# Four building steps' keys compared in one 16-bit operation, and GpSimd's waits moved onto semaphore increments

## The reference, cut to what matters

```python
agg = jax.ops.segment_sum(h[src], dst, num_segments=n)            # convolution
msgs = transformed[etypes, src]                                    # recurrent cell, 4 edge types
a = jax.ops.segment_sum(msgs, dst, num_segments=num_nodes)
# the message network, per edge, both directions:
edge_in_f = jnp.concatenate([node_states[from_idx], node_states[to_idx], edge_features], axis=-1)
msgs_f = _mlp2(edge_in_f, W1_f, b1_f, W2_f, b2_f)
agg = agg + jax.ops.segment_sum(msgs_r, from_idx, num_segments=n_nodes)
```

## Time and profile before

| | us |
|---|---|
| median of 3 runs | 14334.22 (14333.57 to 14341.42) |
| the profiled execution | 14337.0 |
| its span, first to last instruction | 14335.3 |
| busy: PE, DVE, POOL, ACT | 11014.9, 6087.1, 4602.6, 3500.8 |
| building, first step's product to the last | 334.8 to 3152.2 |
| message stage, GpSimd's first gather to its last scatter | 4649.6 to 10099 |

### The profile page before, as it was taken

How to read it: one execution, slowest core, us unless ns; L and a number is a source line. 1 busy time by engine, 2 the same in 40 slices (tenths; PEclk the granted TensorE clock), 3 DMA queues, 4 the chain that set the end, 5 groups by cost and what they waited for, 6 DMA issues and landing times.

```text
span 14335.3 us, 276563 instructions
## 1 busy us (share of the span) xinstructions
PE 11014.9 (77%) x60459; PEld 6477.5 (45%) x60460; DVE 6087.1 (42%) x28514; ACT 3500.8 (24%) x9549; POOL 4602.6 (32%) x4343
## 2 busy tenths in 40 slices
PE   2666666659997777676776767677789999999999
PEld 2333333333333555555555555555644444444443
DVE  6999999875653333333333333333210000000000
ACT  0545455543330222222222222222100000000000
POOL 2000000000000788888888888888100000000000
PEclk8667766769998899999999999999599999999999
DMA  2333333342216233333333333333589899899898
GB/s 92 116 112 116 112 116 112 112 127 85 98 72 266 37 41 42 41 42 41 41 41 41 41 41 41 41 41 41 44 314 342 327 344 341 329 342 344 328 340 301
DMA packets 1120446, 2096.56 MB, mean 146 GB/s; under 512 B 372941, under 2 KB 982880, under 8 KB 1012496
## 3 DMA queue, kind: packets, MB, share of 16 engines
q1 hardware_dynamic: 823736, 1913.57, 37.9%
q0 software_dynamic: 295904, 174.34, 11.5%
HBM read 1630.27 MB, written 457.23 MB: 146 GB/s over the span
## 4 chain that ended last, share of the span: by engine, by line
PE 50%; issue 21%; POOL 15%; DVE 9%; DMA 1%; DVEq 1%; SPq 1%; ACT 1%; POOLq 0%; ACTq 0%; another core or an unknown queue 0%
PE ps L1484 16%; POOL G L493 8%; PE ps L1489 8%; PE ps L1132 7%; POOL reverse L816 6%; PE ps L1187 4%; DVE hots L1810 2%; DVE hots L1812 2%; PE ps L1178 2%; DVE hots L1811 2%; PE ps L1426 1%; PE ps L1336 1%; PE ps L1287 1%; POOL scatter_hold L815 1%; DMA reverse<-SD,sidx 1%
## 5 line engine op out<-in xcount | busy, mean ns | idle before, releaser
L816 POOL DMA_INDIRECT reverse<-SD,sidx x1660 | 2653.9, 1599 | 389.7 <-issue 378.4
L1132 PE MATMUL ps<-hots 128*128 128x392 f16 x4859 | 1711.4, 441 | 1108.5 <-DVE hots L1812 567.7
L1484 PE MATMUL ps<-chunk,feat 128*128 128x512 f16 (+1 forms) x10192 | 2278.9, 375 | 14.4 <-DVE feat L2161 13.4
L493 POOL DMA_INDIRECT G<-h_table,idx x1660 | 1654.4, 997 | 493.2 <-issue 490.4
L2015 DVE TENSOR_TENSOR acc<-acc,ps 128x132 f32 x1660 | 484.6, 292 | 3094.3 <-PE ps L1350 3014.0
L846 ACT ACTIVATE stagebuf<-ps 128x392 f32 x3248 | 1439.5, 508 | 1414.2 <-PE ps L1135 1347.4
L1347 PE MATMUL ps<-MS,OH 128*128 128x128 f32 x3320 | 781.3, 319 | 1256.2 <-issue 910.9
L1484 PEld LDWEIGHTS ps<-chunk,feat 128*128 128x128 bf16 x10192 | 942.9, 98 | 1342.7 <-issue 349.5
L2121 DVE SCALAR_TENSOR_TENSOR gate_t<-ps,early,gate_rz 64x512 f32<-64x512 f32 (+1 forms) x52 | 37.1, 713 | 3228.1 <-ACT gate_rz L992 3228.1
L1812 DVE TENSOR_SCALAR hots<-count_hi,key_hi 128x294 f16<-128x294 f16 x4859 | 1401.3, 288 | 0.0
L923 ACT ACTIVATE SD<-ps 128x129 f32<-128x129 f32 x1660 | 463.2, 279 | 3803.2 <-DMA reverse<-SD,sidx 3792.6
(11 more groups left out here) (418 smaller groups left out, 15179.4 us busy)
## 6 DMA issues: line engine op xcount, KB each, us to landing
chunk<-adj SPq DMA_DIRECT2D x720, 1792.0 KB, 9.0
adj<-stagebuf SPq DMA_DIRECT2D x406, 784.0 KB, 5.6
chunkA<-adj SPq DMA_DIRECT2D x48, 1792.0 KB, 6.7
chunk<-adj SPq DMA_DIRECT2D x60, 1232.0 KB, 6.9
G<-in_edge SPq DMA_DIRECT2D x1660, 32.0 KB
G<-h_table,idx POOLq DMA_INDIRECT x1660
reverse<-SD,sidx POOLq DMA_INDIRECT x1660
reverse<-acc SPq DMA_DIRECT2D x4, 3225.0 KB, 20.0
```

Source lines behind the costliest of these rows:

```text
L493: nc.gpsimd.indirect_dma_start(G[:, j, 0:width], None, table, bass.IndirectOffsetOnAxis(idx[:, j:j + 1], 0))\
L816: nc.gpsimd.indirect_dma_start(reverse[j % R], bass.IndirectOffsetOnAxis(sidx[:, j:j + 1], 0), SD[:, j % R, :], None, compute_op=ALU.add). ...
L1132: nc.tensor.matmul(ps[:, bass.ds(held["banks"][j % STEPW] >> 12, 2 * COMBS)], hots[:, j % BRING, 0:P], hots[:, j % BRING, P:P + 2 * COMBS] ...
L1484: nc.tensor.matmul(bank[k % 2][:, 0:cols], feat[0][:, hi, 0:2, :].rearrange("p a d -> p (a d)"), columns(chunk4, i % DRING, m, cols), star ...
```

## The change

VectorE handles four steps at once. The ring holds four groups of four steps, with the four steps as the innermost dimension: the element for column c of step s lies at place 4c + s. Keys and counts are 16-bit floats; the counts are repeated four times in SBUF. Three `tensor_tensor` comparisons a group, of 512, 392 and 1176 elements, take the place of twelve `tensor_scalar`; the second operand is four keys, read again for each column. TensorE reads stationary and moving columns with a step of four elements (8 bytes). The key without its type is made in 16 bits. `hot_made` counts groups. On GpSimd both dummy operations become a semaphore increment, without a wait for their own predecessor; the other waits stay.

```diff
+HG = 4
+HGROUPS = -(-BSTEPS // HG)
+HRING = BRING // HG
...
-        key_u = early[:, 0:BPAD]
+        key_u = early[:, 0:BPAD // 2].bitcast(F16)
...
-        key_lo = here("key_lo", [P, BPAD])
-        key_hi = here("key_hi", [P, BPAD])
+        key_lo = here("key_lo", [P, BPAD], F16)
+        key_hi = here("key_hi", [P, BPAD], F16)
...
-        count_lo = here("count_lo", [P, P], F16)
-        count_hi = here("count_hi", [P, 2 * COMBS], F16)
+        count_lo = here("count_lo", [P, P, HG], F16)
+        count_hi = here("count_hi", [P, 2 * COMBS, HG], F16)
...
-        hots = here("hots", [P, BRING, P + 2 * COMBS], F16)
+        hots = here("hots", [P, HRING, P + 2 * COMBS, HG], F16)
...
-        hots_f = stagebuf[:, 0:2 * BPAD].bitcast(F32)
+        hots_f = stagebuf[:, 0:BPAD]
...
-                    pool.wait_ge(gather_go, turns + (it * 2 + half) + 1)
-                    nc.gpsimd.tensor_tensor(hold_out[:, :], hold_in[:, :], hold_in[:, :], ALU.add)\
-                        .then_inc(gather_go, 1)
+                    pool.sem_inc(gather_go, 1)
...
-            sp.wait_ge(hot_made, BSTEPS)
+            sp.wait_ge(hot_made, HGROUPS)
...
-                    if not (known(k) and k < 1):
-                        pool.wait_ge(scatter_go, k // 2 if known(k) else it * (UP // 2) + j // 2)
-                    nc.gpsimd.tensor_tensor(scatter_hold[:, :], hold_in[:, :], hold_in[:, :], ALU.add).then_inc(scatter_go, 1)
+                    pool.sem_inc(scatter_go, 1)
...
-                    pe.wait_ge(hot_made, min(k + BATCH, BSTEPS) if known(k) else k + BATCH)
+                    pe.wait_ge(hot_made, it * (SWEEP // HG) + j // HG + 1)
...
-                nc.tensor.matmul(ps[:, bass.ds(held["banks"][j % STEPW] >> 12, 2 * COMBS)], hots[:, j % BRING, 0:P],
-                                 hots[:, j % BRING, P:P + 2 * COMBS],
+                nc.tensor.matmul(ps[:, bass.ds(held["banks"][j % STEPW] >> 12, 2 * COMBS)], hots[:, j // HG % HRING, 0:P, j % HG],
+                                 hots[:, j // HG % HRING, P:P + 2 * COMBS, j % HG],
...
-            link(copy_(count_lo[:, :], iota16[:, 1:P + 1]))
-            link(copy_(count_hi[:, :], iota16[:, 0:2 * COMBS]))
+            link(copy_(count_lo[:, :, :], iota16[:, 1:P + 1].unsqueeze(2).to_broadcast([P, P, HG])))
+            link(copy_(count_hi[:, :, :], iota16[:, 0:2 * COMBS].unsqueeze(2).to_broadcast([P, 2 * COMBS, HG])))
...
+            def keys_of(keys, k, columns):
+                return part(keys[:, :], k, HG).unsqueeze(1).to_broadcast([P, columns, HG])
...
-                if not (known(k) and k < BRING):
-                    v.wait_ge(step_done, k - BRING + 1)
-                nc.vector.tensor_scalar(hots[:, j, 0:P], count_lo[:, :], part(key_lo[:, :], k, 1), None, ALU.is_equal)
-                nc.vector.tensor_scalar(hots[:, j, P:P + 2 * NB], count_hi[:, 0:2 * NB], part(key_u, k, 1), None, ALU.is_equal)
-                nc.vector.tensor_scalar(hots[:, j, P + 2 * NB:P + 2 * COMBS], count_hi[:, 2 * NB:2 * COMBS],
-                                        part(key_hi[:, :], k, 1), None, ALU.is_equal).then_inc(hot_made, 1)
-            pipeline(v, BSTEPS, BRING, 0, lambda it, j: stage(BSTEPS, BRING, it, j, 0, hots_of))
+                if not (known(k) and k < HRING):
+                    v.wait_ge(step_done, k * HG - BRING + HG)
+                nc.vector.tensor_tensor(hots[:, j, 0:P, :], count_lo[:, :, :], keys_of(key_lo, k, P), ALU.is_equal)
+                nc.vector.tensor_tensor(hots[:, j, P:P + 2 * NB, :], count_hi[:, 0:2 * NB, :], keys_of(key_u, k, 2 * NB), ALU.is_equal)
+                nc.vector.tensor_tensor(hots[:, j, P + 2 * NB:P + 2 * COMBS, :], count_hi[:, 2 * NB:2 * COMBS, :],
+                                        keys_of(key_hi, k, 2 * COMBS - 2 * NB), ALU.is_equal).then_inc(hot_made, 1)
+            pipeline(v, HGROUPS, HRING, 0, lambda it, j: stage(HGROUPS, HRING, it, j, 0, hots_of))
```

More of the change, by code:

```diff
@@ L192, in build @@
         hold_in = sb("hold_in", [P, 1])
-        hold_out = sb("hold_out", [P, 1])
-        scatter_hold = sb("scatter_hold", [P, 1])
         hold2 = sb("hold2", [P, 1])
@@ L733, in _ @@
                                     pattern=[[-1, P]], channel_multiplier=1).then_inc(consts, 1)
-            nc.gpsimd.tensor_tensor(hold_out[:, :], hold_in[:, :], hold_in[:, :], ALU.add).then_inc(gather_go, 1)
             pool.wait_ge(tiles_known, 1)
```

## The result

| | before | after |
|---|---|---|
| median, us (4 runs each, same chip) | 14336.26 (14333.57 to 14341.42) | 14238.49 (14232.44 to 14244.76) |
| profiled execution; span | 14337.0; 14335.3 | 14236.6; 14234.8 |
| start to building's first product | 334.8 | 322.0 |
| building, first product to last | 2817.4 | 2814.7 |
| from there to the first gather | 1498.0 | 1497.3 |

The ratio is 0.9931, 95% interval 0.9914 to 0.9949; 14245 had been predicted. Of the 100.5 us between the spans, 88.8 come from the message stage, 12.8 from the start and 2.7 from building.

A forecast was written before the change was run, and what follows sets the result against it. TensorE with its sequencer's reads was taken to bound building, GpSimd the message stage. Terms -12 + 1 - 66 - 12 + 0 = -89 took 14337 to 14248, and 3 us for the median gave 14245 us; range 14200 to 14330.

The forecast's parts named there:

- Building is bound by TensorE and its sequencer's reads: Building stage: TensorE's products, about 0.36 us each, and its sequencer's reads set the length; building stays near 2817 us.
- The comparisons: VectorE in building: 1.27 us a group, 1000 us less VectorE work, worth 0 on the path.
- Rival 1: Building: comparisons run at one element a cycle, VectorE sets the pace at 2854 to 2890 us; 14310 us, 9%.
- The 8-byte step: TensorE's strided reads in building: no slower than before, taken as 0 from row L1298.
- if L1132 becomes longer: Sign against the prediction: TensorE's product in building taking longer than its earlier pitch of 0.36 us.
- the penalty: TensorE's strided reads in building: a small slowdown showing at full clock alone, some +50 us, 14295 us, 4%.
- Rival 2: Building: the strided operand halves TensorE's read rate, +1069 us, 15315 us, 8%.
- The key table and the first group: Before building: 16-bit key table passes save 12 us; the first group, ready later, costs 1 us.
- Scatter and gather waits: GpSimd in the message stage: increments for holds save 66 us at 830 scatters and 12 us at 83 gathers.
- Rivals 3 and 4: GpSimd's message stage: 3, increments bring nothing, 14323 us, 8%; 4, they hold up the queue, +274, 14597 us, 4%.
- Rival 5: Building: VectorE does bound it, as the profile's waits say, losing 257 us; 13988 us, 5%.

The follow-up runs named there:

- the layout by steps: Changed kernel with a 64-byte unused tile, ring laid out by steps, key still along the innermost axis, TensorE reading adjacent elements: 14343.72 us, ratio 1.0014.

## Why the prediction was right, step by step

- *Building is bound by TensorE and its sequencer's reads.* Shown. What moved building moved the sum of the reads by nearly as much (41 and 41 us, 196 and 198, 162 and 153), and a third less work on VectorE moved it by 3. The sum of the parts was -89 us, and the spans differ by 100.5; nearly all of what is missing is GpSimd's.
- *The comparisons.* 0.43, 0.36 and 0.77 us, as worked out from the float32 rows and L1659. The overlap held too: 1.27 us a group were forecast, and the first groups, which wait for nothing, start 1.29 us apart. Later ones start 1.50 us apart because TensorE does, which is the cover that the prediction spoke of. VectorE's busy time in building is 1672 us, within the 1700 named. The rule of the Trainium skill ("Vector Engine (DVE) Microarchitecture Reference", section 5.1) agrees with both traces: four keys side by side, 0.51 ns an element; one key repeated, 1.04. Rival 1 is what the layout by steps does, though at 2936 us and not 2854 to 2890: its three operations take 2.70 us, not 2.62, a group starts 2.37 us after the other, not 2.35, and VectorE idles 58 us.
- *The 8-byte step.* **This step failed**, though its term held. I took 0 for the product from L1298, which was too short a read to show a pace. The product of 392 columns starts each 0.374 us at either clock; with adjacent elements it was 0.310 at 2.4 GHz and 0.354 at 1.2. The step costs 0.06 us a product at full clock and 0.02 at half, 114 us inside the batches. By my own list ("if L1132 becomes longer") the prediction would be wrong here. The time came out by luck in this term: the penalty, for which the prediction had 4% and +50 us, cost the stage nothing because the pauses of the sequencer took it in, and the prediction had not reckoned with that. The Trainium skill ("Advanced Engine Details and Errata", SBUF Cachelines) lets two hits on each 16-byte line go at full rate; the traces disagree, 0.374 against 0.31 us. Rival 2 was to decide "as soon as a column costs more than at present at half clock". It does cost more, 0.02 us a product, and building kept its length all the same: not only the size of the rival was wrong, but also its assumption that products alone are the pace at half clock.
- *The key table and the first group:* -11 predicted, -12.8 measured. The seven passes take 1.43 and 2.69 us where 1.48 and 2.68 were forecast.
- *Scatter and gather waits:* -78 predicted, -88.8 measured in the stage: 79 and 9 by the distances, 66 and 12 predicted. The prediction had read one distance of each kind; the means differ by 0.095 us for a scatter hold and not 0.08, and by 0.1 for a gather hold and not 0.15. What lies behind the stage grew by 5 us; in the other kernels it lies between 4235 and 4243 us without a pattern. Rivals 3 and 4 (increments that bring nothing or hold up the queue) fall with the gaps of 0.30.
- *Rival 5*, the waits taken at their word, would have given 257 us; building gave 3. The label moved to "issue" for the most part, and what the pauses lost went into slower products.
- *What the sum didn't have:* that taking two tiles of 4 bytes away shifts `stagebuf`. Here it moved from one bad start to another (96 and 64 bytes past a multiple of 128), so the change neither won nor lost by it; a start on a multiple would have brought 41 us more in building, 47 in all by the ratios (0.9931 against 0.9898).

What stays open: the padding moves other tiles as well, so it is inferred, from the stores' reading it, that `stagebuf`'s own start is what shortens the bursts; and why words 16 bytes apart take a sequencer so long.

## What to carry to other kernels

Ask of each long pause what the engine's own sequencer does in it before you believe the releaser: here all register reads together were 940 us of a stage of 2817, 198 us of them removable with one copy of a table row, while 883 us less work on the busiest-looking engine gave 3. An edit that is free only under another bound's cover (the 8-byte step) should be priced as if the cover were gone. After removing or adding even a tiny tile, look where the large DMA sources now start.

## What the runs showed of the hardware that was not expected

- A read of 16 adjacent words from SBUF by TensorE's sequencer takes 1.10 to 1.28 us alone and up to 4.1 beside a store (2.4 to 2.8 on average); of 16 words 16 bytes apart 3.8 alone, and up to 7.3 beside one.
- A store of 896-byte pieces takes 4.67 to 4.80 us a burst from a tile that starts on a multiple of 128 bytes and 4.96 from one at 32, 64 or 96 past it.
- A product of 128 and 392 columns, both read with a step of four 2-byte elements, starts each 0.374 us at both clocks, instead of 0.310 and 0.354.
- Two indirect transfers of GpSimd are 0.30 us apart, and a one-column operation between them adds only 0.1.
- A jump back of TensorE's hardware loop costs 0.4 us.
